# Scoring two heads of each batch a step sooner, in a two-layer cross-attention kernel

## What is computed

```python
q = split_heads(layernorm(x) @ Wq + bq)
k = split_heads(ctx @ Wk + bk)
v = split_heads(ctx @ Wv + bv)
scores = einsum('bhqd,bhkd->bhqk', q, k) / sqrt(16)
scores = where(mask, -1e15, scores)          # layer 0 alone has a mask
attn = softmax(scores, axis=-1)
x = x + tanh(g_xattn[0]) * (einsum('bhqk,bhkd->bqhd', attn, v).reshape(b, s, d) @ Wo + bo)
...
x = x + tanh(g_ffn[0]) * moe(layernorm(x))
x = x + tanh(g_xattn[1]) * attention_1(layernorm(x), ctx)
x = x + tanh(g_ffn[1]) * dense_with_lora(layernorm(x))
```

## Time and profile before

| | |
|---|---|
| median of 3 runs | 873.31 us (873.05, 873.31, 881.18) |
| profiled execution, span from the first to the last instruction | 871.8 us |
| PE busy | 781.5 us, 90% |
| DVE busy | 580.9 us, 67% |
| ACT busy | 472.6 us, 54% |
| POOL busy | 213.6 us, 24% |
| attention steps of layer 0 | 17 to 18 us each, some 57 to 331 us |
| attention steps of layer 1 | 16 to 19 us each, some 493 to 766 us |

### The profile page before, as it was taken

How to read it: one execution, slowest core, us unless ns; L and a number is a source line. 1 busy time by engine, 2 the same in 40 slices (tenths; PEclk the granted TensorE clock), 3 DMA queues, 4 the chain that set the end, 5 groups by cost and what they waited for, 6 DMA issues and landing times.

```text
span 871.8 us, 22331 instructions
## 1 busy us (share of the span) xinstructions
PE 781.5 (90%) x7992; PEld 603.7 (69%) x7992; DVE 580.9 (67%) x1773; ACT 472.6 (54%) x1012; POOL 213.6 (24%) x212
## 2 busy tenths in 40 slices
PE   5879999999999888999996599999999989888996
PEld 2546777777777665689974476766776667577996
DVE  3777777777787767764545777778788667564333
ACT  2445566566555556356652355655566555654553
POOL 2553132133222406500035522422221111000000
PEclk9899999999999999899998799999999999899999
DMA  7598788868876905623327958798689887000001
GB/s 200 141 225 201 152 157 174 159 147 175 171 166 139 214 17 147 178 93 121 123 77 165 186 128 152 148 190 178 134 182 186 165 170 159 10 1 1 20 19 38
DMA packets 153755, 117.87 MB, mean 135 GB/s; under 512 B 81564, under 2 KB 145160, under 8 KB 153640
## 3 DMA queue, kind: packets, MB, share of 16 engines
q1 hardware_dynamic: 146400, 107.93, 57.5%
q0 software_dynamic: 4096, 6.57, 3.1%
q10 hardware_dynamic: 3152, 1.96, 0.8%
HBM read 76.17 MB, written 38.30 MB: 131 GB/s over the span
## 4 chain that ended last, share of the span: by engine, by line
PE 56%; DMA 15%; SPq 11%; DVE 7%; ACT 5%; issue 4%; ACTq 1%; POOL 0%; DVEq 0%
PE ps L1963 18%; PE ps L2081 7%; DMA cT<-in_ctxT 6%; PE ps L2107 5%; PE ps L2130 4%; PE ps L2140 4%; DMA scr_q<-qp 4%; SPq L477 3%; DMA QS<-mp 3%; PE ps L2126 2%; PE ps L2401 2%; PE ps L2164 2%; SPq L426 2%; DMA QS<-scr_q 2%; SPq L413 2%
## 5 line engine op out<-in xcount | busy, mean ns | idle before, releaser
L1018 ACT ACTIVATE prob<-ps 128x400 f32<-128x400 f32 (+1 forms) x384 | 182.7, 500 | 95.4 <-PE ps L2130 88.8
L2107 PE MATMUL ps<-KS,QS 96*100 96x361 bf16 x512 | 166.9, 342 | 18.1 <-DMA QS<-scr_q 6.2
L1576 DVE CUSTOM_DVE_ANT_0 ps<-ps,biasq 100x361 f32<-100x361 f32 x256 | 135.3, 543 | 54.1 <-PE ps L2107 50.7
L1580 DVE TENSOR_REDUCE mx<-ps 100x1 f32<-100x361 f32 x256 | 127.0, 527 | 57.8 <-PE ps L2107 56.7
L2130 PEld LDWEIGHTS ps<-QS,KS 98*128 98x128 bf16 x1536 | 110.5, 101 | 53.0 <-issue 9.8
L2130 PE MATMUL ps<-QS,KS 98*128 98x100 bf16 x1536 | 135.2, 212 | 8.7 <-ACT prob L1018 4.4
L2081 PE MATMUL ps<-cT,wk 128*128 128x361 f32 x256 | 98.6, 496 | 17.5 <-DMA cT<-in_ctxT 9.9
L2107 PEld LDWEIGHTS ps<-KS,QS 96*100 96x100 bf16 x512 | 64.3, 127 | 54.9 <-DVE mx L1580 14.1
L728 POOL TENSOR_TENSOR kp<-kr,kp 128x722 bf16<-128x722 f32 x32 | 48.7, 1523 | 193.0 <-ACT kp L989 192.7
L2140 PE MATMUL ps<-prob,V 128*17 128x100 f32 (+1 forms) x3072 | 79.8, 252 | 0.2 <-ACT xT L909 0.2
L2140 PEld LDWEIGHTS ps<-prob,V 128*17 128x17 f32 (+1 forms) x3072 | 64.4, 98 | 11.9 <-issue 8.7
(11 more groups left out here) (225 smaller groups left out, 1609.3 us busy)
## 6 DMA issues: line engine op xcount, KB each, us to landing
scr_k<-kp SPq DMA_DIRECT2D x93, 180.5 KB, 5.2
KS<-scr_k SPq DMA_DIRECT2D x62, 270.8 KB, 3.8
cT<-in_ctxT SPq DMA_DIRECT2D x32, 361.0 KB, 5.2
KS<-scr_k SPq DMA_DIRECT2D x62, 180.5 KB, 4.1
QS<-scr_q SPq DMA_DIRECT2D x60, 150.0 KB, 4.2
KS<-scr_k SPq DMA_DIRECT2D x62, 90.2 KB, 4.4
scr_q<-qp SPq DMA_DIRECT2D x42, 100.0 KB, 6.0
xg<-scr_x SPq DMA_DIRECT2D x32, 128.0 KB
```

The source lines that it names most:

```text
L1018: nc.scalar.activation(prob[0:KROWS[t], t, hg, :], ps[0:KROWS[t], c % 2, 0:HQ * S], ACT.Exp).then_inc(a["exp"], 1)
L1576: nc.vector.tensor_tensor_reduce(ps[0:S, banks[h % len(banks)], 0:S2], ps[0:S, banks[h % len(banks)], 0:S2], biasq[p][:, :], 1.0, -3.0e38, ...
L1580: nc.vector.reduce_max(mx[:, h:h + 1], ps[0:S, banks[h % len(banks)], 0:S2], axis=AX.X).then_inc(a["max"], 1)
L2107: mm(ps[0:S, banks[h % len(banks)], 0:S2], QS[p][0:SROWS, h, :], KS[p][0:SROWS, h * S2:(h + 1) * S2], start=True, stop=True).then_inc(a["s ...
```

## The change

Nothing is computed that was not computed before. What moves:

- Heads 0 and 1 of batch b + 2 are scored at the end of step b, between the three value tiles, which are now all three there (`score_ahead`, `AHEAD = 2`). `last_values` is gone. Step b scores heads 2 to 15 of batch b + 1, each at a place two heads further on; VectorE takes the two maxima of batch b + 2 after `k_rest` and before statistics and `combine`.
- The second part of the key projection is cut in two and put between the last score_T tiles, with `turn_max` before the last two of these.
- SyncE loads the context of batch b + 4 at the end of step b, ahead of the key stores of batch b + 3, where it loaded the context of batch b + 3 at the start of step b, behind the key stores of the step before.
- The six query stores of layer 1 are made in odd steps: three after `max_load`, three behind the key stores.

```diff
@@ SyncE: step @@
-                if has_ctx and b > 0:
-                    ctx_load(l, b + 3, 1 - u, False)
-                if l == 1 and u == 0 and 2 <= b <= 12:
-                    q_store(l, b // 2 + 1)
                 if has_k:
                     k_load(l, b + 2, 0)
                     q_load(l, b + 2, 0)
...
                     max_load(l, b + 1, 1 - u)
+                    if l == 1 and u == 1 and b <= 11:
+                        q_store(l, (b + 3) // 2, range(NST // 2))
                     sp.wait_ge(sd["mload"][1 - u], 16 * (i + u + 1))
                     sp.sem_inc(s_held, 1)
                     k_load(l, b + 2, 1)
                     q_load(l, b + 2, 1)
+                    if b + 4 < B:
+                        ctx_load(l, b + 4, u, False)
...
                 if has_ctx:
                     k_store(l, b + 3)
+                if l == 1 and u == 1 and b <= 11:
+                    q_store(l, (b + 3) // 2, range(NST // 2, NST))
@@ VectorE: step @@
-                for h in range(H):
+                for h in range(AHEAD, H):
                     if has_b:
                         maxima(l, b + 1, 1 - u, h, h + 1, SBANKS)
-                    between(l, b, u, h)
-                    if has_o and h == 2:
+                    between(l, b, u, h - AHEAD)
+                    if has_o and h == 3:
                         divide(l, b - 1)
-                    if has_o and h == 8:
+                    if has_o and h == 10:
                         add_attention(l, b - 1)
...
                 if has_k:
                     k_rest(l, b + 3, 1)
+                if has_2:
+                    maxima(l, b + 2, u, 0, AHEAD, SBANKS)
                 if has_o:
                     stats(2 * l + 1, b - 1, sa[l]["x"], b)
@@ TensorE: step @@
+                def score_ahead(h):
+                    if has_2:
+                        if h == 0:
+                            pe.wait_ge(d["kload"][0][u], loaded(l, b + 2))
+                        score(l, b + 2, u, h, SBANKS)
...
-                next_score(0)
-                next_score(1)
+                next_score(2)
                 if has_o:
                     turn_o(l, b - 1, b)
...
                 for t in range(NKT):
                     score_T(l, b, u, 0, t)
-                    if t < 2:
-                        next_score(2 + t)
-                last_values()
+                    next_score(3 + t)
                 if has_o:
                     turn_on(l, b - 1)
...
                 for t in range(NKT):
-                    next_score(4 + t)
+                    next_score(6 + t)
                     score_T(l, b, u, 1, t)
-                next_score(7)
+                next_score(9)
...
-                next_score(15)
-                if has_k:
-                    project_k(l, b + 3, 1 - u, i + 1 + u, 1)
-                score_T(l, b, u, 3, 1)
+                keys(1, 0)
                 if has_b:
                     turn_max(l, b + 1, b, 7)
+                score_T(l, b, u, 3, 1)
+                keys(1, 1)
                 score_T(l, b, u, 3, 2)
...
                 for hg in range(1, NHG):
                     weigh(l, b, u, hg)
-                for t in range(NKT - 1):
+                for t in range(NKT):
                     values(t)
+                    if t < AHEAD:
+                        score_ahead(t)
```

More of the change, by code:

```diff
@@ L29 @@
 SBANKS0 = (2, 3, 0, 1)
+AHEAD = 2
 K2_AT = ((3, 5), (7, 8))
@@ L470, in q_load, with q_store @@
                              scr_q[half, :, :, n * S:(n + 1) * S].rearrange("r (d h) n -> (r d) h n", h=HH)).then_inc(sd["kload"][half][p], 16)
-            def q_store(l, g):
+            def q_store(l, g, rows=range(NST)):
                 u, nb, t0 = g % 2, GB if l == 0 else 2, 1 if g == 0 else 0
                 q = sq[u]
-                for r in range(NST):
+                for r in rows:
                     queries_split(l, g, QPART[r])
@@ L1749, in attn @@
                     fold_biases()
+                maxima(l, 1, 1, 0, AHEAD, SBANKS)
                 step(l, 0, 0, l * IB, False, True, True, True)
@@ L2171, in next_score, with keys @@
                     if has_b:
-                        if h % HH == 0:
-                            pe.wait_ge(d["kload"][h // HH][1 - u], loaded(l, b + 1))
+                        if h == HH:
+                            pe.wait_ge(d["kload"][1][1 - u], loaded(l, b + 1))
                         score(l, b + 1, 1 - u, h, SBANKS)
+                def keys(m, k):
+                    if has_k:
+                        project_k(l, b + 3, 1 - u, i + 1 + u, m, (k,))
                 def values(t):
@@ L2180, in values @@
                             project_v(l, b + 2, u, t, k, b + 3 if has_k else None)
-                def last_values():
-                    if has_o and has_b:
-                        for k in range(KT):
-                            project_v(l, b + 1, 1 - u, NKT - 1, k, b + 2 if has_2 else None)
-                next_score(0)
-                next_score(1)
+                def score_ahead(h):
[4 more added lines that the diff above has]
+                next_score(2)
                 if has_o:
@@ L2219, in step @@
                     norm(F1N, 0)
-                next_score(8)
+                next_score(10)
                 if l == 0 and u == 1 and 3 <= b < B - 1:
@@ L2242, in step @@
                     logits(l, 0)
-                for k in range(KT):
-                    if has_k:
-                        project_k(l, b + 3, 1 - u, i + 1 + u, 0, (k,))
-                    next_score(13 + k)
+                keys(0, 0)
+                next_score(15)
+                keys(0, 1)
                 score_T(l, b, u, 3, 0)
-                next_score(15)
-                if has_k:
-                    project_k(l, b + 3, 1 - u, i + 1 + u, 1)
-                score_T(l, b, u, 3, 1)
+                keys(1, 0)
                 if has_b:
                     turn_max(l, b + 1, b, 7)
+                score_T(l, b, u, 3, 1)
+                keys(1, 1)
                 score_T(l, b, u, 3, 2)
@@ L2338, in attn @@
                     pe.wait_ge(s_gates, 1)
+                pe.wait_ge(sd["kload"][0][1], loaded(l, 1))
+                for h in range(AHEAD):
+                    score(l, 1, 1, h, SBANKS)
                 step(l, 0, 0, l * IB, False, True, True, True)
```

4 lines of the change are left out of this document (2 added, 2 removed).

## The result

The changed kernel takes 890.73 us (885.57, 888.81, 892.66, 895.04), the kernel before 873.62 us with one more run: a ratio of 1.019, 95% interval 1.0145 to 1.0235. The profiled execution took 885.57 us, with a span of 883.4 us against 871.8: +11.6 us, where the prediction's sum was +10.8. It is the fastest of the four, so the trace shows some 5 us less than the medians differ by.

A forecast was written before the change was run, and what follows sets the result against it. VectorE's chain was taken to bound the head part of odd steps, with TensorE's work there as cover. Costs of +10.4, +11 and +7.4 make +28.8, less 18: +10.8 us, so 884 us; range 860 to 893.

The forecast's parts named there:

- Context waits go: TensorE's waits for context loads (9.9 us by matmuls, 12.8 by weight loads) go; below 2 us in all left.
- Query-load waits go: TensorE's waits for query loads (6.2 us by matmuls, 7.5 by weight loads) go; below 3 us left.
- waits removed: TensorE's context and query waits together: between 16.1 and 20.3 us gained, taken as 18, some 3 in layer 0.
- The value tile: Third tile moved to the step before: each tail 0.77 us longer; head part gives back between all and less than nothing.
- Odd steps of layer 0: Head part grows by 0.5 us; with the tail 1.3 a step; 18.8 to 19.2 us from the fifth on.
- Even steps of layer 0: Cost about 0.3 us with counts and logits, 0.55 without; steps at 17.4 to 17.6 us.
- Even steps of layer 1: Largest term: VectorE starts 2.0 us after the first score, before 0.7; 2.2 us for each of steps 2 to 10: 11.
- Odd steps of layer 1: Nothing given back: 0.77 us for six steps, 7.4 with the ends; steps at 17.2 to 17.6 us.
- Waits for maxima and xn up by 15 us or more: TensorE's waits for VectorE's maxima (at scores) and for xn rise by 15 us or more.
- Rival 1: TensorE bounds everywhere, head parts shrink by the tile, only the waits go: 855 us; chance 0.15.
- Rival 2: The delay is there but half the size, 14.4 us less 18: 870 us; chance 0.25.
- Rival 3: The ring of loads becomes the bound: some 897 us; sign, TensorE waiting for a load at the early score; chance 0.10.

The follow-up runs named there:

- tile only: The kernel before with one edit, the third value tile computed at the end of the step and no longer in the next head part: 878.45 us, 1.0029.
- heads ahead: The changed kernel with the third value tile back in the head part and context loads back in their place: 886.23 us, 1.0144.
- the second trace: Trace of the changed kernel run again, unaltered, on the third chip: 890.17 us, 1.0234 times the kernel before.
- the combine first: The changed kernel with statistics and combine ahead of the two early maxima on VectorE: 874.89 us on the second chip, 1.0152 times the kernel before.
- the division first: The changed kernel with VectorE's division behind the step's first maximum, not its second: 880.17 us on the second chip, 1.0230 times the kernel before.
- the kernel with both orders mended: The changed kernel with combine ahead of the first two maxima and division ahead of the fourth head's maximum: 881.22 us, 1.0095 times the kernel before.
- the fastest one: The kernel before with three query stores in the odd step behind the maxima's load, three in the even step behind its context load: 865.05 us, 0.9941.

## Why the prediction was right

The forecast of 884 and its direction held; the measured 890.7 is 6.8 above it and inside the range. The mechanism of the largest term is there, but the sum came out so near by luck, as terms on both sides were too large. By its steps:

- **Context waits go**: right (0.3 us left), but not for the reason given alone. Some 7 us of them go with the tile (tile only: 3.2 and 5.7 us left), and where scores wait for VectorE they are hidden (heads ahead: 1.7 and 2.2 left, with the context load in its old place).
- **Query-load waits go**: wrong in sum; 8.4 and 7.4 us are left (5.2 and 6.1 in the second trace). Right for the steps 1 to 11 of layer 1, where 1.8 us went; the other waits in the line lie elsewhere, and I had put them down to the query stores too. The term "waits removed" was 18 and is 8 to 13 by the first trace (9.9 by the matmuls, less the 2.2 that their query line rose, and 12.8 by the weight loads, whose query line did not rise), and 11 to 14 by the second.
- **The value tile**: +0.77 us a tail, of which VectorE's chain gives nothing back. Right in layer 0 (tile only: +6.3 us, some 0.5 us a step). In even steps of layer 1 it is some 0.4: with the combine first they are 16.14 us, before 15.7 without waits for loads, so there the head part gives part of it back.
- **Odd steps of layer 0**: forecast 1.3 each to 18.8 to 19.2; measured 18.38, some 0.5 us a step over the steps before. The third head's maximum starts 1.46 us into the step (256.43 on 254.97), as worked out (1.48), but the head part did not grow by 0.5; it shrank from 6.74 to 6.26 (the normalization's second transpose is at 261.23). The division now follows two maxima of the step and not three (the rows of order ahead of the prediction show it; I used it nowhere), and `bsc` took 0.17 us.
- **Even steps of layer 0**: forecast 17.4 to 17.6, measured 17.72. The division is too late here: 0.3 with the division first.
- **Even steps of layer 1**: the mechanism exact (1.93 for 2.0 us, a third score that waits 1.20), the size 1.6 us a step (17.35 for 15.7) and not 2.2: 1.2 for the late start, 0.4 for the tile.
- **Odd steps of layer 1**: forecast +0.77 and 17.2 to 17.6 us, measured 16.88 against 16.42 where nothing else waits: +0.46.
- **Waits for maxima and xn up by 15 us or more**: only by some 7 (`mx` of L1583 from 1.2 to 7.2 us by the matmuls, from 14.1 to 21.2 by the weight loads; xn from 5.7 to 6.3). The rest of VectorE's lateness shows as onv, from 2.5 to 9.2 us, which I had not listed.
- **turn_max costs nothing**: right for the time, though a line of 13.3 us appeared.
- **Not in the forecast at all: the clock.** At the same matmuls an even step of layer 1 with a stretch of 3.4 us at the lower clock takes 18.19 to 19.10 us, one without 17.35: 0.8 to 1.75 us. In steps 1 to 13 of layer 1 there are two such stretches before, and four in each trace of the changed kernel. By these prices two more are 1.7 to 3.5 us (an estimate), more than half or all of the 2.8 us that the steps 1 to 13 grew; without them costs and removed waits would nearly cancel in layer 1. What brought them is not shown. On the third chip the mean granted clock of all runs is 0.963 before and 0.954 after; 0.009 of 888 us is 8 us, at most that, as some of it falls where TensorE has little to do.

So errors in size cancelled, by luck: the waits removed were put 5 to 10 us too high, and the steps' costs, 28.8, are 20 to 25 (11.6 and the 8 to 13 removed), with the clock in them. The sum of +10.8 against +11.6 is better than its terms, and it is nearer to this fastest trace than to the medians, which differ by 17.1. Rival 1 (TensorE bounds) is refuted by the waits for `mx` and onv. The section of the Trainium skill that the prediction names beside it ("Perfetto Trace Analysis", "Identifying the Most-Contended Engine") takes the share of weight loads, not of matmuls, for TensorE: 69% against VectorE's 67%, which hardly chooses between the two. Rival 2, half the costs, lies below what was measured; in the odd steps alone it is about right (0.5 for 1.3 in layer 0, 0.46 for 0.77 in layer 1). Rival 3 did not come in the changed kernel: no first or early score of the steps 1 to 11 of layer 1 waits for a load, and the key stores leave sooner than before. Its sign, TensorE at a step's first score for a load, came in the three kernels in which the contexts move and the scores do not; in two of them since the load waits for the third tile, not for its bytes.

What stays open: the 0.95% that is left in the kernel with both orders mended is not split between tail, loads and clock, and that kernel was not run with the query stores placed as in the fastest one.

## What to carry to other kernels

Before work is moved sooner on the engine that waits, follow the engine that takes it over through the same place: what stands behind it there starts later, here by 1.2 us a step for one combine. A DMA put ahead of others in a queue holds them for as long as it waits itself, so look for the last reader of its buffer (34.0 us of queue wait against 5.5). Do not add a removed wait to a new cost ahead of it in the same step: what comes later anyway no longer waits. And try an edit in parts: three query stores on the right side of one load made the kernel 0.6% faster, on the wrong side 1.8% slower.

## What the runs showed of the hardware

In these traces TensorE's clock also fell to its lower level in the middle of stretches in which it was busy for most of the time, behind short waits. In the changed kernel, the 4.17 us ahead of a fall and the 3.41 us behind it, then the same places of step 8, where the clock stayed (columns: window, length, busy time of PE, PEld, DVE, ACT and POOL, clock, DMA share, GB/s):

```profile
536.35:540.52 4.17, 3.02 (x26) 1.97 (x26) 4.13 (x12) 2.52 (x6) 3.08 (x4) 1.00 1.10 245
540.52:543.93 3.41, 3.41 (x29) 2.30 (x32) 1.59 (x5) 1.20 (x2) 0.00 (x0) 0.50 0.94 143
641.90:646.07 4.17, 3.22 (x27) 2.11 (x28) 4.13 (x12) 2.52 (x6) 0.94 (x2) 1.00 1.07 246
646.07:649.48 3.41, 3.31 (x48) 2.28 (x48) 2.78 (x7) 2.10 (x4) 0.00 (x0) 1.00 1.01 132
```

TensorE was idle for 1.15 us of the first and for 0.95 us of the third window, and at half clock (1.2 GHz, 2.4 before) it ran 29 matmuls where it ran 48. The Trainium skill, "TensorE: Matmul & The Clock Gate", "HAM oscillation — how this bites in real kernels", describes falls behind waits for a DMA of some 3 to 5 us; here the longest wait in the first window is 1.21 us, and it is for VectorE (`mx` of L1583). Why one of two nearly equal stretches is followed by a fall is not shown. The lower clock explains why steps alike in instructions came out in two lengths (16.14 and 17.66 to 18.32 us, at mean clocks of 1.00 and of 0.90 to 0.91). If a wait brings a fall about, it is worth more than its line; that it does is not shown.
